# Three expert stages: router in column groups, Sinkhorn with one exponential, small loads during the norm, first weights ahead of the scatters

## The chip, the cores and the metric

The program runs on one core of a Trainium2 chip. The metric is the time of one execution on the device in microseconds. The kernel before took 3872.72 us (median of 3 runs, 3868.19 to 3879.06).

The core has TensorE (PE in the profile; its weight loads PEld), VectorE (DVE), ScalarE (ACT), GpSimd (POOL) and SyncE (SP). Each runs its own list of instructions in order; semaphores order them among each other. Transfers are issued from SP and from POOL and carried by 16 DMA engines. Everything is in fp32; large products are made from operands that are split into a high and a low part.

## The reference

The input x is two sequences of 1024 tokens of 256 features. Eight layers follow, each of the form `x = x + f(layernorm(x))`: a cross attention (A), experts (B), a cross attention (C), experts (D), a cross attention (E), a self attention with experts (F), a time warping alignment (G) and soft experts (H). The change touches the three expert layers. Each has 8 experts and chooses for every token one (B) or two (D, F):

```python
# B: top 1
logits = xf @ Wg + bg
gates = softmax(logits); idx = argmax(gates)
h = gelu(einsum('th,ehi->tei', xf, W1) + b1); y = einsum('tei,eih->teh', h, W2) + b2
out = y[token, idx]
# D: top 2 of Sinkhorn gates
scores = (einsum('btd,ed->bte', x, router_w) + router_b) / max(temperature, 0.1)
for _ in range(3):
    log_alpha = log_alpha - logsumexp(log_alpha, axis=-1, keepdims=True)   # over experts
    log_alpha = log_alpha - logsumexp(log_alpha, axis=-2, keepdims=True)   # over tokens
gates = exp(log_alpha); gates = gates / (sum(gates, axis=-1) + 1e-8)
topk_vals, topk_idx = top_k(gates, 2)
topk_gates = topk_vals / (sum(topk_vals) + 1e-8)
out = x + sum_k topk_gates[k] * (relu(x @ wg[e]) * (x @ wp[e])) @ wo[e]     # e = topk_idx[k]
# F: top 2 of the logits
rw, sel = top_k(xf @ gate_w.T, 2); rw = softmax(rw)
out = sum_k rw[k] * ((silu(xf @ w1[e].T) * (xf @ w3[e].T)) @ w2[e].T)       # e = sel[k]
```

## The kernel before

x and y hold the 2048 tokens with their features on the partitions (`[128, 2, 2048]`). The program is a row of stages; between two of them all engines meet at a barrier. The layernorm of a layer is a stage of its own (`norm_stage`, four blocks of 512 tokens), the experts the next (`moe`, names B, D, F). `norm_stage` can issue DMAs given to it as `early` from SP while it computes; before, only layer H uses that.

A `moe` stage goes through these steps:

1. **Small loads.** SP issues 8 to 10 small DMAs (router weights, index constants, bias), line 779. PE waits for all of them.
2. **Router.** PE makes the logits with the tokens as weights: 16 tiles of 128 tokens, 2 halves of the features, 8 columns each (line 836). fp32 products are issued as two instructions, so that the profile shows 64. PE then transposes the tokens into token order (line 845), and ACT copies them to `y_tok` (line 1136).
3. **Choice.** DVE, one small step after another with a semaphore between them (`chain`), makes scores and the one-hot choice. Stage D runs three Sinkhorn rounds first (lines 959 to 975): maxima over experts, exponential, sum, logarithm, subtraction, then the same over tokens, with the maximum over partitions on POOL (line 802) and the sum over partitions on PE (line 850). Exponentials and logarithms are done by ACT on request (`act_does`, line 1132), in order behind its copies to `y_tok`.
4. **Places.** PE counts the choices before each token (lines 852, 853), DVE works out which slot of 256 places belongs to which expert and each token's place (lines 1004 to 1033).
5. **Scatter.** POOL writes the tokens to their places in DRAM by indirect DMAs, 16 of them in B, 32 in D and F (line 809). Ahead of them it fetches the first slot's weights (line 795), behind them the second and third; `raw` has room for 3 slots.
6. **Slots.** 15 slots in B, 23 in D and F. SP loads a slot's tokens once all scatters have landed (line 776), PE transposes them (line 863), ACT and DVE split tokens (lines 1152, 1062) and weights (lines 1161, 1068, in pieces of 1024 columns: 1 in B, 3 in D and F), PE multiplies (lines 879, 894), POOL writes the result back by indirect DMAs (line 816) and fetches the weights of the slot three ahead. Then the results are gathered and added to x.

What sets the order is the order of the code on each engine, written by hand, and the semaphores. PE transposes slots 0 and 1 before it multiplies slot 0.

Of the kernel before, what the change touches and what calls it, by code (L numbers as in the profile page):

```python
# [656 lines left out]
def moe(nc, name, kind, func, hidden, pairs, consts, x, y, t, plus):  # L657
# [21 lines left out]
    BT = BLK // P  # L679
    rounds = 3 if kind == "sinkhorn" else 0  # L680
# [3 lines left out]
    with ExitStack() as stack:  # L684
        sc = Scope(nc, stack, name)
        router_w = sc.sb("router_w", [P, C, E])
# [12 lines left out]
        if kind == "sinkhorn":  # L699
            temp_t = sc.sb("temperature", [P, 1])  # L700
            small.append((temp_t[:, :], t[f"{name}_temperature"]))
            temperature = temp_t[:, 0:1]
        score, left, index, keep, expd = (sc.sb(n, wide) for n in ("score", "left", "index", "keep", "expd"))
# [28 lines left out]
        names = """small_loaded logits_ps dve_step act_asked act_done maxima_ready maxima_all sums_ready sums_all  # L732
# [37 lines left out]
        @block.sync  # L770
        def _(sp):
            def load(i):
                if i >= LOADS:
                    sp.wait_ge(s["turned_ps"], i - LOADS + 1)
                    sp.wait_ge(s["dest_ready"], i - LOADS + 1)
                sp.dma_start(tile_in[:, i % LOADS], rows_of(slots_dram, i)).then_inc(tile_loaded[i % LOADS], 16)

            for dst, src in small:
                sp.dma_start(dst, src).then_inc(s["small_loaded"], 16)
# [12 lines left out]
        @block.gpsimd  # L792
        def _(pool):
            def fetch(i):
                pool.indirect_dma_start(out=raw[:, i % RAWS, :], out_offset=None, in_=w_rows,
                                        in_offset=bass.IndirectOffsetOnAxis(ap=row_of[:, i:i + 1], axis=0))\
                    .then_inc(raw_loaded[i % RAWS], 16)

            pool.memset(ones_n[:, :], 1.0).then_inc(s["ones_ready"], 1)
            for r in range(rounds):  # L800
                pool.wait_ge(s["maxima_ready"], r + 1)
                pool.partition_all_reduce(colv[:, 1, :], colv[:, 0, :], P, bass.bass_isa.ReduceOp.max).then_inc(s["maxima_all"], 1)
            pool.wait_ge(s["rows_ready"], 1)
            fetch(0)
            pool.wait_ge(s["slots_ready"], 1)
            pool.wait_ge(s["tok_ready"], TILES // 2)
            for k in range(K):
                for n in range(TILES):
                    pool.indirect_dma_start(out=slots_dram, in_=y_tok[:, n, :], in_offset=None,
                                            out_offset=bass.IndirectOffsetOnAxis(ap=slot_of[:, k * TILES + n:k * TILES + n + 1], axis=0))\  # L810
                        .then_inc(scattered, 16)
            def store(i):
                pool.wait_ge(s["z_ready"], i + 1)
                pool.wait_ge(s["dest_ready"], i + 1)
                for h in range(H):
                    pool.indirect_dma_start(out=made_dram, in_=z[:, i % ZS, h, :], in_offset=None,
                                            out_offset=bass.IndirectOffsetOnAxis(ap=dest_of[:, i, h:h + 1], axis=0))\
                        .then_inc(z_stored[i % ZS], 16)

            for i in range(1, SLOTS):  # L820
                if i >= RAWS:
                    pool.wait_ge(s["w_lo_ready"], PIECES * (i - RAWS + 1))
                    if biased:
                        pool.wait_ge(s["z_ready"], i - RAWS + 1)
                fetch(i)
                if i >= RAWS:
                    store(i - RAWS)
            for i in range(SLOTS - RAWS, SLOTS):
                store(i)

        @block.tensor
        def _(pe):
            pe.wait_ge(s["small_loaded"], 16 * len(small))
# [89 lines left out]
        def _(dve):  # L923
# [21 lines left out]
            dve.wait_ge(s["small_loaded"], 16 * len(small))  # L945
            dve.wait_ge(s["logits_ps"], 1)
            logits = ps[:, 0, 0:TILES * E].rearrange("p (t e) -> p t e", e=E)
            if bias is not None:
                step(dve.tensor_tensor(score[:, :, :], logits, bias.unsqueeze(1).broadcast_to(wide), ALU.add))
            else:  # L950
                step(dve.tensor_copy(score[:, :, :], logits))
            if kind == "sinkhorn":
# [3 lines left out]
                step(dve.tensor_scalar(score[:, :, :], score[:, :, :], temp[:, 1:2], None, ALU.mult))  # L956
                for r in range(rounds):

                    step(dve.tensor_reduce(rowv[:, 0, :], score[:, :, :], AX.X, ALU.max))
                    step(dve.tensor_tensor(score[:, :, :], score[:, :, :], per_token(rowv[:, 0, :]), ALU.subtract))  # L960
# [3 lines left out]
                    step(dve.tensor_tensor(score[:, :, :], score[:, :, :], per_token(rowv[:, 2, :]), ALU.subtract))  # L964

                    step(dve.tensor_reduce(grouped(colv[:, 0, :]), s4, AX.X, ALU.max))
                    dve.sem_inc(s["maxima_ready"], 1)
                    dve.wait_ge(s["maxima_all"], r + 1)
                    step(dve.tensor_tensor(s4, s4, per_expert(colv[:, 1, :]), ALU.subtract))
                    act_does()  # L970
                    step(dve.tensor_reduce(grouped(colv[:, 3, :]), by_expert(expd[:, :, :]), AX.X, ALU.add))
                    dve.sem_inc(s["sums_ready"], 1)
                    dve.wait_ge(s["sums_all"], r + 1)
                    act_does()
                    step(dve.tensor_tensor(s4, s4, per_expert(colv[:, 4, :]), ALU.subtract))
                act_does()
# [119 lines left out]
            lo(0)  # L1096
            for j in range(PIECES):
                w_lo(0, j)
            lo(1)
# [29 lines left out]
        def _(act):  # L1129
# [3 lines left out]

            for n in range(TILES // 2):
# [3 lines left out]
            for r in range(rounds):  # L1138
                answer(4 * r + 1, expd[:, :, :], score[:, :, :], ACT.Exp)
                answer(4 * r + 2, rowv[:, 2, :], rowv[:, 1, :], ACT.Ln)  # L1140
                answer(4 * r + 3, expd[:, :, :], score[:, :, :], ACT.Exp)
                answer(4 * r + 4, colv[:, 4, :], ps[:, 1, 0:G], ACT.Ln)
            if kind == "sinkhorn":
                answer(4 * rounds + 1, expd[:, :, :], score[:, :, :], ACT.Exp)
# [39 lines left out]
            hi(0)  # L1184
            for j in range(PIECES):
                w_hi(0, j)
            hi(1)
# [1281 lines left out]
def program(nc, t, out):  # L2469
# [5 lines left out]
    with ExitStack() as stack:  # L2475
# [36 lines left out]
        norm_stage(nc, "nB", consts, norm_jobs(x, y))  # L2512
        moe(nc, "B", "top1", ACT.Gelu, D, 1, consts, x, y, t, [])
# [3 lines left out]
        norm_stage(nc, "nD", consts, norm_jobs(x, y))  # L2517
        moe(nc, "D", "sinkhorn", ACT.Relu, 2 * D, 2, consts, x, y, t, [y])
# [5 lines left out]
        with ExitStack() as layer:  # L2524
# [6 lines left out]
            norm_stage(nc, "nF2", consts, norm_jobs(y, r, scale=lnw["ln2_w"]), rms=True)  # L2531
            moe(nc, "F", "top2", ACT.Silu, 2 * D, 2, consts, x, r, t, [y])
# [12 lines left out]
def lay_out(np, i):  # L2545
# [4 lines left out]
    def rows(w):  # L2550
        return w.reshape(-1, P, w.shape[-1]).transpose(1, 0, 2)

# [31 lines left out]
    t["B_router_w"], t["B_router_b"] = rows(i["L0_ffn_Wg"]), everywhere(i["L0_ffn_bg"])  # L2584

    experts("D", [i["L1_ffn_wg"], i["L1_ffn_wp"]], i["L1_ffn_wo"])
    t["D_router_w"], t["D_router_b"] = rows(i["L1_ffn_router_w"].T), everywhere(i["L1_ffn_router_b"])
# [4 lines left out]
    t["F_router_w"] = rows(i["L2_ffn_gate_w"].T)  # L2592
# [69 lines left out]
```

## Time and profile before

| | |
|---|---|
| median of 3 runs | 3872.72 us (3868.19 to 3879.06) |
| the profiled execution | 3867.78 us, span 3865.9 us |
| mean granted clock of TensorE | 0.873 of 2.4 GHz |
| PE, DVE, ACT, POOL busy | 2975.2, 2120.6, 1513.0, 1001.7 us |
| stage B from its first small load to the end of its weights' use | 1203.4 to about 1376 us |
| stage D, the same | 1583.5 to about 1937 us |
| stage F, the same | 2804.3 to about 3130 us |
| norm ahead of stage D | 1561.7 to 1583.2 us |
| the 23 slots of stage D (lines 879, 894) | 1705.6 to 1936.5 us |
| router products (line 836) | 64 in each stage, 13.8 us in each |
| stretches before the first expert product | 61.5 us in B, 122.1 us in D, 94.4 us in F |

The profiled execution's own time is 1.9 us over its span. The last row is the time from the first small load to the first product of line 879. A fetch or scatter is an indirect DMA that POOL issues; its row on POOL is the issuing, not the transfer. Row times are counted from the start of the span. A timeline row is start, duration, engine, line, operation and operands; what stands in brackets is the idle time of the engine before it and what ended it.

### The profile page before, as it was taken

The numbers are of one execution on the slowest core, as the hardware profiler recorded it, in microseconds if no ns is written. First come the engines' busy times: TensorE is split into PE (matmuls) and PEld (weight loads), VectorE is DVE, ScalarE is ACT, GpSimd is POOL, SyncE is SP. The second block draws the span as 40 slices with busy tenths as digits, with TensorE's granted clock in tenths as the row PEclk, the third lists the DMA queues.
The fourth block names the chain that finished last, engine by engine and source line by source line (L and its number), as shares of the span: only waits on it lengthen the run. The fifth ranks groups of instructions, "written<-read, shape, count | busy, mean of one in ns | idle before, by whom it ended". The sixth has DMA issues, their size and how long they took to land. (4 is left out here: it accounts for less than half of the span.)

```text
span 3865.9 us, 43438 instructions
## 1 busy us (share of the span) xinstructions
PE 2975.2 (77%) x15086; PEld 1758.0 (45%) x15086; DVE 2120.6 (55%) x3884; ACT 1513.0 (39%) x2113; POOL 1001.7 (26%) x600
## 2 busy tenths in 40 slices
PE   4899999999994668439978599899629961049989
PEld 1545454545443542339942233333229950024457
DVE  3656555555532434338725378788327836853365
ACT  2344444444442423326523245555505630012254
POOL 1356565655572310043300100000133311001100
PEclk7899999999996788669988689999859985569999
DMA  2020000000020420045410000000025621000060
GB/s 72 5 64 7 6 6 2 4 6 6 0 66 30 150 61 1 3 151 218 174 58 1 11 4 1 6 5 2 1 106 196 217 76 17 4 22 18 37 218 22
DMA packets 87114, 198.34 MB, mean 51 GB/s; under 512 B 20387, under 2 KB 62755, under 8 KB 78880
## 3 DMA queue, kind: packets, MB, share of 16 engines
q0 software_dynamic: 18480, 108.86, 7.8%
q1 hardware_dynamic: 64608, 83.27, 7.2%
q10 hardware_dynamic: 3856, 3.95, 0.5%
q8 instruction: 105, 1.72, 0.2%
q14 instruction: 65, 0.53, 0.0%
HBM read 146.02 MB, written 49.76 MB: 51 GB/s over the span
## 5 line engine op out<-in xcount | busy, mean ns | idle before, releaser
L621 POOL TENSOR_TENSOR A_key_sums<-A_key_sums,A_probs 128x1024 f32<-128x1024 f32 (+1 forms) x224 | 526.9, 2371 | 228.1 <-ACT A_probs L514 228.1
L514 ACT ACTIVATE A_probs<-A_banks 128x512 f32<-128x512 f32 (+1 forms) x576 | 329.1, 597 | 384.7 <-PE A_banks L434 382.4
L564 DVE TENSOR_REDUCE A_part_max<-A_banks 128x1 f32<-128x367 f32 x768 | 354.1, 530 | 156.9 <-PE A_banks L355 155.6
L1844 DVE TENSOR_REDUCE F_part_max<-F_banks 128x1 f32<-128x512 f32 x512 | 325.3, 685 | 61.7 <-PE F_banks L1697 59.0
L1790 ACT ACTIVATE F_probs<-F_banks 128x1024 f32<-128x1024 f32 x256 | 248.3, 1023 | 240.5 <-PE F_banks L1743 240.3
L383 PE MATMUL A_banks<-A_probs,A_v_tok 128*64 128x512 f32 x1152 | 278.7, 605 | 0.0
L432 PE MATMUL A_banks<-A_q_one,A_k_one 128*128 128x512 f32 (+1 forms) x576 | 255.5, 444 | 26.2 <-ACT A_probs L514 23.1
L355 PE MATMUL A_banks<-A_k_one,A_q_one 128*128 128x368 f32 x768 | 230.3, 383 | 6.8 <-ACT A_v_tok L494 6.5
L184 POOL TENSOR_SCALAR F_r<-F_r,F_ln_w 128x512 f32<-128x512 f32 x16 | 28.8, 1812 | 783.0 <-DVE F_r L149 783.0
L434 PE MATMUL A_banks<-A_q_two,A_k_two 128*128 128x512 f32 (+1 forms) x576 | 227.1, 394 | 0.0
L355 PEld LDWEIGHTS A_banks<-A_k_one,A_q_one 128*128 128x128 f32 x768 | 147.3, 192 | 94.6 <-DVE A_part_max L564 58.5
L2122 PE MATMUL G_banks<-G_path_rows,G_ctx_hi 77*128 77x512 f32 x8 | 5.2, 645 | 226.0 <-DMA G_path_rows<-align_path 226.0
L432 PEld LDWEIGHTS A_banks<-A_q_one,A_k_one 128*128 128x128 f32 (+1 forms) x576 | 106.0, 184 | 139.0 <-issue 97.2
L1697 PE MATMUL F_banks<-F_k_split,F_q_split 64*128 64x512 f32 x512 | 157.3, 489 | 7.6 <-DVE F_part_max L1844 5.8
L2283 POOL TENSOR_TENSOR H_diff<-H_logits 128x512 f32<-128x512 f32 x32 | 40.7, 1272 | 426.8 <-DVE H_logits L2259 415.6
L309 PE MATMUL A_banks<-g_y,A_wqkv 128*128 128x512 f32 x256 | 121.9, 621 | 30.7 <-DVE A_part_max L604 26.0
L1710 PE MATMUL F_banks<-F_probs,F_v_tok 128*32 128x512 f32 x1024 | 143.0, 632 | 2.1 <-ACT F_probs L1790 1.9
L621 POOL TENSOR_TENSOR A_key_sums<-A_probs 128x1024 f32<-128x1024 f32 x32 | 76.0, 2375 | 261.7 <-ACT A_probs L514 261.7
L879 PE MATMUL F_banks<-F_y_hi,F_w_split 128*128 128x256 f32 x736 | 129.6, 289 | 14.4 <-DVE F_w_split L1068 14.4
L879 PE MATMUL D_banks<-D_y_hi,D_w_split 128*128 128x256 f32 x736 | 129.2, 288 | 14.4 <-DVE D_w_split L1068 14.4
L1743 PE MATMUL F_banks<-F_q_split,F_k_split 64*128 64x512 f32 x512 | 131.5, 464 | 11.0 <-ACT F_probs L1790 5.7
L1697 PEld LDWEIGHTS F_banks<-F_k_split,F_q_split 64*128 64x128 f32 x512 | 72.2, 195 | 134.0 <-DVE F_part_max L1844 102.2
(577 smaller groups left out, 6357.8 us busy)
## 6 DMA issues: line engine op xcount, KB each, us to landing
Hm_staged<-in_H_w SPq DMA_DIRECT2D x6, 1024.0 KB, 5.5
moe_in_D<-A_zeros SPq DMA_DIRECT2D x1, 6003.0 KB, 25.8
moe_in_F<-A_zeros SPq DMA_DIRECT2D x1, 6003.0 KB, 25.3
D_tile_in<-moe_in_D SPq DMA_DIRECT2D x23, 261.0 KB, 5.1
F_tile_in<-moe_in_F SPq DMA_DIRECT2D x23, 261.0 KB, 5.1
H_phi<-in_H_w SPq DMA_DIRECT2D x5, 1024.0 KB, 5.6
H_w<-in_H_w SPq DMA_DIRECT2D x5, 1024.0 KB, 4.9
D_y_tok<-moe_out_D SPq DMA_DIRECT2D x8, 512.0 KB, 5.5
```

The costliest lines, as they stand in the source:

```text
L355: pe.matmul(ps[:, MAX_BANKS[i % 3], 0:PW], q_one[:, b, j, qt * P:(qt + 1) * P], k_one[:, b, j, (i % 3) * PIECE:(i % 3) * PIECE + PW], star ...
L383: mm = pe.matmul(ps[DH * j:DH * j + DH, 4 + blk, :], v_tok[:, b, kt, DH * j:DH * j + DH], probs[:, j, kt % RING, blk * BLK:(blk + 1) * BLK ...
L432: pe.matmul(ps[0:kw, half % 3, :], k_one[:, b, j, kt * P:kt * P + kw], q_one[:, b, j, cols], start=True, stop=False)
L434: pe.matmul(ps[0:kw, half % 3, :], k_two[:, b, j, kt * P:kt * P + kw], q_two[:, b, j, cols], start=False, stop=True).then_inc(s["score_ps" ...
L514: act.activation(probs[0:kw, j, kt % RING, blk * BLK:(blk + 1) * BLK], ps[0:kw, half % 3, :], ACT.Exp, scale=1.0 / 8.0).then_inc(s["exp_re ...
L564: dve.tensor_reduce(part_max[:, i // 3, i % 3:i % 3 + 1], ps[:, MAX_BANKS[i % 3], 0:PIECE], AX.X, ALU.max).then_inc(s["piece_max"], 1)
L621: pool.tensor_tensor(key_sums[0:kw, j, :], before, probs[0:kw, j, kt % RING, :], ALU.add).then_inc(s["summed"], 1)
L879: mm = pe.matmul(ps[:, 1 + pairs * (n % 2) + pair, at * SLOT:(at + 1) * SLOT], weight_in(i, w_part, pair, c, QM * q + at), part[:, i % 2, ...
L1697: mm = pe.matmul(bank, q_split[rr, b, qt * P // BLK, hd // 2, qt * P % BLK:qt * P % BLK + P], k_split[rr, b, hd // 2, kb * BLK:(kb + 1) * ...
L1710: mm = pe.matmul(ps[V0 * hd:V0 * hd + V0, 7, :], v_tok[:, b, kt, V0 * hd:V0 * hd + V0], probs[:, i % RING, hd, :], start=kt == 0, stop=kt ...
L1790: act.activation(probs[:, i % RING, heads_at, :], ps[:, heads_at, :], ACT.Exp, scale=DH ** -0.5).then_inc(s["exp_ready"], 1)
L1844: op = dve.tensor_reduce(part_max[:, maximum_at(hd, qt), kb:kb + 1], bank, AX.X, ALU.max)
```

## The change

In all three expert stages:

- **Small loads** are handed to the norm stage ahead, whose SP block issues them. For this `moe` now calls the norm itself.
- **Router.** The weights are now `router_w`, padded from 8 to 32 columns, and the tokens are streamed, 512 columns at a time. The four blocks of tokens go to four column groups of the array and so to four groups of 32 partitions of one bank. The logits then stand as expert by token; ACT copies them to SBUF, and PE turns them with four transposes, which stand behind the first four token transposes.
- **Sinkhorn** (D). The maxima over experts and over tokens are subtracted once, one exponential is taken, and the three rounds divide by sums (reciprocal and product on DVE). One request to ACT and one to POOL are left.
- **First weights.** POOL fetches slots 0 and 1 ahead of the scatters and slot 2 in the middle of them. ACT and DVE split slot 0's weights before they wait for the first tokens. POOL's fetch of slot 3 then needs only this split (and in B, as before, the first result).

The core of the diff:

```diff
@@ moe, scope
+        small_loaded = sc.sem("small_loaded")
+        norm([(dst, src, small_loaded) for dst, src in small])
@@ POOL
-            for r in range(rounds):
-                pool.wait_ge(s["maxima_ready"], r + 1)
+            if rounds:
+                pool.wait_ge(s["maxima_ready"], 1)
                 pool.partition_all_reduce(colv[:, 1, :], colv[:, 0, :], P, bass.bass_isa.ReduceOp.max).then_inc(s["maxima_all"], 1)
             pool.wait_ge(s["rows_ready"], 1)
-            fetch(0)
+            for i in range(RAWS - 1):
+                fetch(i)
             pool.wait_ge(s["slots_ready"], 1)
             pool.wait_ge(s["tok_ready"], TILES // 2)
             for k in range(K):
                 for n in range(TILES):
+                    if k * TILES + n == KT // 2:
+                        fetch(RAWS - 1)
...
-            for i in range(1, SLOTS):
-                if i >= RAWS:
-                    pool.wait_ge(s["w_lo_ready"], PIECES * (i - RAWS + 1))
+            for i in range(RAWS, SLOTS):
+                pool.wait_ge(s["w_lo_ready"], PIECES * (i - RAWS + 1))
@@ PE
-            for n in range(TILES):
-                for c in range(C):
-                    mm = pe.matmul(ps[:, 0, n * E:(n + 1) * E], y[:, c, n * P:(n + 1) * P], router_w[:, c, :],
+            for c in range(C):
+                for g in range(NBLK):
+                    mm = pe.matmul(ps[g * ER:(g + 1) * ER, 0, :], router_w[:, c, :], y[:, c, g * BLK:(g + 1) * BLK],
                                    start=c == 0, stop=c == C - 1)
-            mm.then_inc(s["logits_ps"], 1)
+            mm.then_inc(s["by_expert_ps"], 1)
             for n in range(TILES // 2):
+                if n == 1:
+                    pe.wait_ge(s["by_expert_ready"], 1)
+                    for i in range(BT):
+                        mm = pe.transpose(ps[:, 1, i * P:(i + 1) * P], logits_t[:, i * P:(i + 1) * P], consts["ident"][:, :])
+                    mm.then_inc(s["logits_ps"], 1)
@@ DVE, Sinkhorn
+                dve.wait_ge(s["maxima_all"], 1)
+                step(dve.tensor_tensor(s4, s4, per_expert(colv[:, 1, :]), ALU.subtract))
+                act_does()
                 for r in range(rounds):
                     step(dve.tensor_reduce(rowv[:, 1, :], expd[:, :, :], AX.X, ALU.add))
-                    act_does()
...
+                    step(dve.reciprocal(rowv[:, 2, :], rowv[:, 1, :]))
+                    step(dve.tensor_tensor(expd[:, :, :], expd[:, :, :], per_token(rowv[:, 2, :]), ALU.mult))
+                    step(dve.tensor_reduce(grouped(colv[:, 3, :]), e4, AX.X, ALU.add))
                     dve.sem_inc(s["sums_ready"], 1)
                     dve.wait_ge(s["sums_all"], r + 1)
-                    act_does()
-                    step(dve.tensor_tensor(s4, s4, per_expert(colv[:, 4, :]), ALU.subtract))
-                act_does()
+                    step(dve.reciprocal(colv[:, 4, :], ps[:, 1, 0:G]))
+                    step(dve.tensor_tensor(e4, e4, per_expert(colv[:, 4, :]), ALU.mult))
@@ DVE, slots (the same on ACT with hi and w_hi)
-            lo(0)
             for j in range(PIECES):
                 w_lo(0, j)
+            lo(0)
             lo(1)
@@ ACT
+            act.wait_ge(s["by_expert_ps"], 1)
+            act.activation(logits_t[:, :], ps[:, 0, :], ACT.Copy).then_inc(s["by_expert_ready"], 1)
```

**PE in stage D, from the router to the first tokens of the slots.** `g_y` is the normed input, `D_banks` PSUM, `D_hot` the one-hot choice. Before:

```order
L836 MATMUL D_banks<-D_router_w,g_y 128x8 x32
L845 MATMUL D_banks<-g_ident,g_y 128x128 x32
L850 MATMUL D_banks<-D_colv,g_ones 128x16 x3
L852 MATMUL D_banks<-D_hot,D_tri 128x256
L853 MATMUL D_banks<-D_hot,g_ones 128x256
```

After:

```order
L841 MATMUL D_banks<-g_y,D_router_w 32x512 x8
L855 MATMUL D_banks<-g_ident,g_y 128x128 x4
L848 MATMUL D_banks<-g_ident,D_logits_t 128x128 x4
L855 MATMUL D_banks<-g_ident,g_y 128x128 x28
L860 MATMUL D_banks<-D_colv,g_ones 128x16 x3
L862 MATMUL D_banks<-D_hot,D_tri 128x256
```

Thirty-two narrow products become eight wide ones on 32 output rows, and four transposes of the logits stand between the token transposes.

**ACT in stage D, behind the copies to `y_tok`.** Before, one round (the pattern of the last five rows stands three times, and one more exponential closes it):

```order
L1136 ACTIVATE D_y_tok<-D_banks 128x2x256 x8
L1132 ACTIVATE D_expd<-D_score 128x128
L1132 ACT_TABLE_LOAD
L1132 ACTIVATE D_rowv<-D_rowv 128x16
L1132 ACT_TABLE_LOAD
L1132 ACTIVATE D_expd<-D_score 128x128
L1132 ACT_TABLE_LOAD
L1132 ACTIVATE D_colv<-D_banks 128x16
L1132 ACT_TABLE_LOAD
```

After:

```order
L1144 ACTIVATE D_logits_t<-D_banks 128x512
L1147 ACTIVATE D_y_tok<-D_banks 128x2x256 x8
L1141 ACTIVATE D_expd<-D_score 128x128
L1167 ACTIVATE D_w_split<-D_raw 128x1024 x3
L1158 ACTIVATE D_y_hi<-D_banks 128x512 x2
L1180 ACTIVATE D_active<-D_banks 128x512
```

The copy of the logits stands first, one exponential is left, no table load stands here, and slot 0's weights are split ahead of the first tokens.

**POOL in stage D, around the scatters.** `D_raw` are fetched weights, `moe_in_D` the tokens' places in DRAM, `moe_out_D` the results. Before:

```order
L799 MEMSET D_ones_n 128x256
L802 ISA
L802 ISA D_colv<-D_colv 128x16 x3
L795 DMA D_raw<-in_D_w,D_row_of 128x3072
L809 DMA moe_in_D<-D_y_tok,D_slot_of 5888x261 x32
L795 DMA D_raw<-in_D_w,D_row_of 128x3072 x3
L816 DMA moe_out_D<-D_z,D_dest_of 9984x256 x2
```

After:

```order
L806 ISA D_colv<-D_colv 128x16
L799 DMA D_raw<-in_D_w,D_row_of 128x3072 x2
L816 DMA moe_in_D<-D_y_tok,D_slot_of 5888x261 x16
L799 DMA D_raw<-in_D_w,D_row_of 128x3072
L816 DMA moe_in_D<-D_y_tok,D_slot_of 5888x261 x16
L799 DMA D_raw<-in_D_w,D_row_of 128x3072
L823 DMA moe_out_D<-D_z,D_dest_of 9984x256 x2
```

One fetch moves ahead of the scatters and one between them; one is left directly behind them.

## Rows read from the trace of the kernel before

**Rows 1.** Timeline of stage D, norm to first exponential: start, duration, engine.

```profile
1583.48 0.33 SPq L779 DMA_DIRECT2D D_router_w<-in_D_router_w  x1
...
1589.75 13.82 PE L836 MATMUL D_banks<-D_router_w,g_y 128*128 128x8 f32 x64 [14.08 <-DMA D_temperature<-in_D_temperature]
...
1603.42 5.09 PE L845 MATMUL D_banks<-g_ident,g_y 128*128 128x128 f32 x32
...
1609.58 0.28 DVE L962 TENSOR_REDUCE D_rowv<-D_expd 128x16 f32<-128x128 f32 x1 [4.24 <-ACT D_expd L1132]
```

**Rows 2.** Timeline of stages B and F: first small load, first counting product.

```profile
1203.40 0.34 SPq L779 DMA_DIRECT2D B_router_w<-in_B_router_w  x1
...
1228.49 0.39 PE L852 MATMUL B_banks<-B_hot,B_tri 128*128 128x128 f32 x2
...
2804.31 0.34 SPq L779 DMA_DIRECT2D F_router_w<-in_F_router_w  x1
...
2829.26 0.60 PE L852 MATMUL F_banks<-F_hot,F_tri 128*128 128x256 f32 x2
```

**Rows 3.** Timeline of PE in stage C: products in column groups, then full ones.

```profile
1449.56 1.06 PE L1311 MATMUL C_banks<-C_probs,C_v_tok 77*32 77x512 f32 x8
...
1452.93 1.98 PE L1277 MATMUL C_banks<-g_y,C_wq 128*128 128x512 f32 x4
```

**Rows 4.** Windows: PE, PEld, DVE, ACT, POOL busy; then clock, DMA share, GB/s.

```profile
1200.00:1203.40 3.40, 0.00 (x0) 0.00 (x0) 3.13 (x3) 0.02 (x1) 0.00 (x0) 0.52 0.00 0
...
1689.90:1700.40 10.50, 0.00 (x0) 0.00 (x0) 0.07 (x1) 0.00 (x0) 0.96 (x1) 0.50 0.95 361
```

**Rows 5.** Line 1132's table loads in the whole program.

```profile
L1132 ACT ACT_TABLE_LOAD  x12: 1283/1283/1283, 1609.6 to 1628.2; - x12
```

**Rows 6.** Timeline of stage D: a column sum in round 1, and the end of the rounds.

```profile
1613.26 0.38 DVE L971 TENSOR_REDUCE D_colv<-D_expd 128x16 f32<-128x128 f32 x1 [0.43 <-ACT D_expd L1132]
...
1614.54 0.18 ACT L1132 ACTIVATE D_colv<-D_banks 128x16 f32<-128x16 f32 x1
...
1629.87 0.29 DVE L977 TENSOR_REDUCE D_rowv<-D_expd 128x16 f32<-128x128 f32 x1 [1.23 <-ACT D_expd L1132]
```

**Rows 7.** Timeline of stages D and B: scatters and a fetch beside DVE's additions.

```profile
1640.67 1.19 POOL L795 DMA_INDIRECT D_raw<-in_D_w,D_row_of  x1 [14.77 <-DVE D_row_of L1013]
...
1645.85 4.63 DVE L1038 TENSOR_TENSOR g_x<-g_x,g_y 128x1024 f32<-128x1024 f32 x4
...
1646.03 1.94 POOL L809 DMA_INDIRECT moe_in_D<-D_y_tok,D_slot_of  x1 [4.17 <-DVE D_slot_of L1033]
...
1277.98 1.45 POOL L795 DMA_INDIRECT B_raw<-in_B_w,B_row_of  x1 [20.63 <-DVE B_z L1091]
```

**Rows 8.** Timeline of stage D, last scatter to first product.

```profile
1688.74 0.98 POOL L795 DMA_INDIRECT D_raw<-in_D_w,D_row_of  x1 [0.30 <-issue]
1689.92 30.14 SPq L776 DMA_DIRECT2D D_tile_in<-moe_in_D  x6
...
1700.44 1.94 PE L863 MATMUL D_banks<-g_ident,D_tile_in 128*128 128x128 f32 x8 [62.61 <-DMA D_tile_in<-moe_in_D]
...
1702.19 0.69 DVE L1062 TENSOR_TENSOR D_y_lo<-D_banks,D_y_hi 128x512 fp32r<-128x512 f32 x1 [1.04 <-ACT D_y_hi L1152]
...
1705.55 0.79 PE L879 MATMUL D_banks<-D_y_hi,D_w_split 128*128 128x256 f32 x2 [3.17 <-DVE D_w_split L1068]
```

**Rows 9.** Timeline of stage B, the same place, and landing times of line 776.

```profile
1256.63 22.52 SPq L776 DMA_DIRECT2D B_tile_in<-moe_in_B  x7
...
1260.87 1.09 PE L863 MATMUL B_banks<-g_ident,B_tile_in 128*128 128x128 f32 x4 [31.77 <-DMA B_tile_in<-moe_in_B]
...
DMA to landing us min/median/max: 2.7/2.9/6.7
```

**Rows 10.** Landing times of the weight fetches: stage D, then stage B behind its scatters.

```profile
DMA to landing us min/median/max: 6.9/7.5/10.1
...
DMA to landing us min/median/max: 4.6/5.6/6.9
```

More of the change, by code:

```diff
@@ L654, in top_experts, with moe @@
             step(dve.tensor_tensor(left[:, :, :], index[:, :, :], keep[:, :, :], ALU.add))
-def moe(nc, name, kind, func, hidden, pairs, consts, x, y, t, plus):
+def moe(nc, name, kind, func, hidden, pairs, consts, x, y, t, plus, norm):
     K = 1 if kind == "top1" else 2
@@ L679, in moe @@
     BT = BLK // P
+    ER = P // NBLK
     rounds = 3 if kind == "sinkhorn" else 0
@@ L943, in grouped @@
                 return v.rearrange("p (b e) -> p b e", b=B)
-            dve.wait_ge(s["small_loaded"], 16 * len(small))
+            dve.wait_ge(small_loaded, 16 * len(small))
             dve.wait_ge(s["logits_ps"], 1)
-            logits = ps[:, 0, 0:TILES * E].rearrange("p (t e) -> p t e", e=E)
+            logits = ps[:, 1, :].rearrange("p (i g e) -> p g i e", g=NBLK, e=ER)[:, :, :, 0:E]
+            by_block = score[:, :, :].rearrange("p (g i) e -> p g i e", g=NBLK)
             if bias is not None:
-                step(dve.tensor_tensor(score[:, :, :], logits, bias.unsqueeze(1).broadcast_to(wide), ALU.add))
+                step(dve.tensor_tensor(by_block, logits, bias.unsqueeze(1).unsqueeze(1).broadcast_to([P, NBLK, BT, E]), ALU.add))
             else:
-                step(dve.tensor_copy(score[:, :, :], logits))
+                step(dve.tensor_copy(by_block, logits))
             if kind == "sinkhorn":
@@ L1137, in _ @@
                                ACT.Copy).then_inc(s["tok_ready"], 1)
[L1138 to L1142, printed above, removed]
             if kind == "sinkhorn":
-                answer(4 * rounds + 1, expd[:, :, :], score[:, :, :], ACT.Exp)
+                answer(1, expd[:, :, :], score[:, :, :], ACT.Exp)
             if kind == "top2":
@@ L2530, in program @@
             self_attention(nc, consts, y, r, t)
[L2531 to L2532 removed]
+            moe(nc, "F", "top2", ACT.Silu, 2 * D, 2, consts, x, r, t, [y],
+                lambda early: norm_stage(nc, "nF2", consts, norm_jobs(y, r, scale=lnw["ln2_w"]), rms=True, early=early))
         norm_stage(nc, "nG", consts, norm_jobs(x, y))
@@ L2551, in rows, with router @@
         return w.reshape(-1, P, w.shape[-1]).transpose(1, 0, 2)
+    def router(w):
+        return np.pad(rows(w), ((0, 0), (0, 0), (0, P // NBLK - E)))
     def column(v):
@@ L2583, in lay_out @@
             np.broadcast_to(i["L0_ffn_b2"][:, None, :], (E, P, D)))
-    t["B_router_w"], t["B_router_b"] = rows(i["L0_ffn_Wg"]), everywhere(i["L0_ffn_bg"])
+    t["B_router_w"], t["B_router_b"] = router(i["L0_ffn_Wg"]), everywhere(i["L0_ffn_bg"])
     experts("D", [i["L1_ffn_wg"], i["L1_ffn_wp"]], i["L1_ffn_wo"])
-    t["D_router_w"], t["D_router_b"] = rows(i["L1_ffn_router_w"].T), everywhere(i["L1_ffn_router_b"])
+    t["D_router_w"], t["D_router_b"] = router(i["L1_ffn_router_w"].T), everywhere(i["L1_ffn_router_b"])
     t["D_temperature"] = everywhere(i["L1_ffn_temperature"])
@@ L2591, in lay_out @@
     experts("F", [i["L2_ffn_w1"].transpose(0, 2, 1), i["L2_ffn_w3"].transpose(0, 2, 1)], i["L2_ffn_w2"].transpose(0, 2, 1))
-    t["F_router_w"] = rows(i["L2_ffn_gate_w"].T)
+    t["F_router_w"] = router(i["L2_ffn_gate_w"].T)
     t["c_half"] = np.tile(np.repeat(np.eye(2, dtype=np.float32), 16, axis=0), (4, 1))
```

41 lines of the change are left out of this document (17 added, 24 removed).

## The prediction

> **What bounds the kernel now.** The views were read in this order: the page, for the shares of the engines; the timelines of the three expert stages, for what follows what ahead of the slots; the windows, for clock and DMA; and the landing times of the DMAs. PE is busy most of the span, but the change touches little of what keeps it busy. Its places lie where one engine works and the others wait: from the end of the norm to the first expert product, 122.1 us in D, 94.4 us in F, 61.5 us in B by the table. Every instruction there is a link of one chain, and a barrier closes each stage, so a microsecond saved there is saved in full unless a neighbour is late next. The reader is to see four links in D: nothing but small loads for 6.3 us, then 13.8 us of router products [rows 1]; 20.3 us from the first exponential to the end of the rounds [rows 1, 6]; a line of scatters on POOL; and 10.5 us from the first load of a slot to the first transpose, 5.1 us more to the first product [rows 8]. The slots behind them keep their code and are taken as unchanged.
>
> **Small loads.** SP's first small load leaves at 1583.48 and PE starts at 1589.75 [rows 1]. In the norm, some 20 us long, SP has nothing else to do, so the 10 issues are hidden. PE starts at about 1583.5, called T below.
>
> **Router.** Before, 64 narrow instructions take 13.82 us, 0.216 us apart [rows 1]. After, there are 8 products of 512 columns, 16 instructions. In stage C four products with 32 output rows each, 8 instructions, begin 0.89 us ahead of what follows (their row spans 1.06 us with the last one's tail), while 4 instructions of full width take 1.98 us [rows 3], some 0.43 us each without the tail. So 8 grouped instructions take the time of two wide ones: the four column groups run side by side. That was at the high level of the clock. After the norm the granted clock is 0.52 before PE starts [rows 4], so at 1.2 GHz the 16 instructions take four times 0.86, 3.4 us. Bounds: 1.7 us if the clock were high; 13.7 us if the groups did not overlap at the low clock (a rival below). I take 3.4, since the clock falls in the same idle stretch.
>
> What is added is ACT's copy and four transposes. A wait of 0.25 and a copy of 0.6 end at T + 4.3. The four transposes at 0.16 to 0.21 us (32 take 5.09 us, [rows 1]) end at T + 5.2, and DVE has logits at T + 5.5.
>
> **What is late next, stage D.** DVE's way to the exponential is 8 steps of some 0.3 us and POOL's maximum, to T + 8.8. ACT is behind: its request stands behind eight copies to `y_tok` of 0.6 us, the second of which needs tokens transposed after the logits. It ends between T + 10.5 (clock high, ACT's 0.6 us a copy the bound) and T + 12.2 (clock low, 0.86 us a pair of tiles). First sum at T + 10.9 to T + 12.6, taken 11.6. Before it was T + 26.1 [rows 1]. **D gains 14.5** (13.5 to 15.2).
>
> **B and F.** There the chain goes to the counting products, 25.1 us after the first small load in B and 24.95 in F [rows 2]. In B they stand in PE's list behind the token transposes, after at T + 9 to T + 11.2, taken 10.3: **14.8**. In F the choice takes DVE 15 steps of 0.33 us from the logits, 5 us, so T + 10.7 to T + 11.3, taken 10.8, and I take off 0.5 for counting products that may meet the low clock: **13.6**.
>
> **Rounds of D.** Before, from 1609.58 to 1629.87 [rows 1, 6], 20.3 us, with 12 table loads of 1.28 us [rows 5]. After, a round is a sum, a reciprocal and a product (0.3 each with the gap behind it, [rows 6]), a sum over tokens until the sum over partitions can be read (1.28 as from L971 to ACT's reading, [rows 6]), a reciprocal of 0.29 and a product of 0.43: 2.93 us, 8.8 for three. The exponential and the logarithm had alternated and made the loads; one exponential is left and the norm's last function is one too. **D gains 11.5** (10.5 to 12).
>
> **Scatters.** The two fetches ahead fall into the 5 us in which POOL waits for DVE's places, so the second is hidden. The fetch in the middle is not: 0.98 and a gap of 0.30 [rows 8], 1.28 us. Then there is DVE. Its four additions from 1645.85 take 4.63 us, and the scatter of 1646.03 beside them takes 1.94 us, where a fetch alone takes 0.98 [rows 7, 8]. Two such scatters stood there. Slot 0's split, 3 pieces of 1.2 us, now comes right behind these additions, while POOL still scatters; a fetch beside such a piece in B took 1.45 [rows 7]. At half speed 3.6 us cost 1.8 (0 to 1.9). **D and F lose 3.1 each; B,** with one piece, **loses 1.9.**
>
> The row rests on two-operand additions from SBUF, of 1.94 against 0.97. The Trainium skill, "SBUF — State Buffer", section "Who interferes with whom", says that such a `tensor_tensor` takes only the shared read interface, and infers from that that it does not hold up the descriptors that GpSimd writes. By that rule the split would cost the scatters nothing and the time would be 4 us shorter; the trace here speaks against it, and I go by the row.
>
> The transfers themselves are covered: between the first fetch and the last scatter lie 47 us, in which at 361 GB/s [rows 4] 17 MB could move; three fetches of 1.57 MB and 4.3 MB of scattered tokens are 9 MB.
>
> **First tokens.** Before, two fetches are issued at the end of the scatters, beside the first load, which needs 10.5 us from 1689.92; DMA is at 0.95 and 361 GB/s [rows 4, 8]. That is 3.8 MB: both fetches and the loads, so the first tokens land only when both fetches are through. After, one fetch stands there, slot 3's, since slot 0's weights are split long before. Its 1.57 MB and the tile's 0.27 at 361 GB/s are 5.1 us, taken 5.3. Bounds are 2.9 us, B's median landing [rows 9], and 8. **D gains 5.2, F,** which repeats it, **5.0.** In B slot 3's fetch still waits for the first result, so the load is alone: 4.24 us before, 2.9 after [rows 9], **1.3**.
>
> **First product.** Before, it waits 5.1 us from the first transposes for two pieces of weights [rows 8]. After, it waits for the tokens' low part, which ended at 1702.88: **2.6 in D, 2.6 in F.** In B the same count gives 1.5; slot 1's transposes stand ahead of the product, so I take **1.0**.
>
> **The sum.** Start and router 14.5 + 13.6 + 14.8 = 42.9; rounds 11.5; scatters -8.1; first tokens 11.5; first product 6.2: 64.0 us. The profiled execution took 3867.78 us, so it would take 3803.8. It is 4.9 under the median of the three runs. From the median the same sum gives 3808.7. I take 3808. Its own range: all low ends together give 50 us, 3820 from 3870; all high ends 75, 3794. So 3794 to 3821.
>
> **Rivals.**
>
> *The column groups do not overlap.* Stage C's products have 77 rows of weights, these 128, and fp32 needs two instructions each. Then 16 instructions at 0.86 us are 13.7 instead of 3.4, 10.3 lost in each stage: 3839. For it: no row shows 128 rows. Against: rows 3 show fp32 in four groups in one bank. Chance 0.08.
>
> *The tokens' way is hardly shortened.* The fetch of slot 3 is issued ahead of SP's first load, and the first load then still lands late; the fetch in the middle pushes scatters back. The first tokens gain nothing (-11.5) and the scatters lose 3 more in each of D and F: 3826. For it: before, the load was held back by whole fetches. Against: half the bytes. Chance 0.12.
>
> *The change doesn't do what it says in the rounds.* If table loads stay between copy, exponential and the slots' function, 1.28 each, D keeps three or four: 3812. Rows 5 put all 12 in line 1132, and copies in between made none. Chance 0.03, inside the first case's range.
>
> *Slower: weights ahead block POOL.* Place: the scatters in POOL's list behind fetches whose descriptors are still in the queue. If there were no room for a scatter's descriptors until a fetch has landed, each of three fetches would stop the line for its landing, up to 10.1 us in D and F [rows 10] and 6.9 in B: 81 us lost against 64 won, 3890. At the medians, 7.5 and 5.6 [rows 10], the loss is 62 us, about even; from there on it decides. Against: the scatter at 1646.03 was issued 5.4 us after the fetch of 1640.67 [rows 7], inside its landing time, and took no longer than DVE's additions explain. Chance 0.02.
>
> **How the numbers follow.** The forecast has 0.75, with the third rival 0.78; groups 0.08, tokens 0.12, slower 0.02. The forecast's own range reaches to 3821. The token case at 3826 lies near and is taken in, and most of the group case with it: 3792 to 3836 leaves out less than 2 in 10. This measurement can't tell less than 0.3%, 12 us, from no change. Faster by more 0.96, within it 0.02, slower by more 0.02.
>
> **What would show it.** Right: the router's row is some 3.4 us for 16 instructions and starts within 0.5 us of the norm's end; no table load in Sinkhorn, and rounds of 2.9 us; two fetches ahead of `slots_ready`, three or four scatters of 1.9 us in D instead of two; the first transposes 5 us after the first load; the first product 2.5 us behind them; the slots as long as before, 231 us in D. Wrong: a router row of 7 us or more, a first load above 8 us, scatters of 2 us all along, or slots that grew by as much as was saved ahead of them.

## Result and profile after

The changed kernel took 3800.81 us (median of 4 runs, 3797.79 to 3805.84) against 3874.16 for the kernel before (4 runs): ratio 0.9816, 95% interval 0.9801 to 0.9831, which is 65 to 77 us saved. In a later series it was 0.9806 (0.9785 to 0.9828). The forecast was 3808.

The profiled execution after took 3805.84 us, 61.9 under that of before. In the page PE's instructions fell from 15086 to 14954, ACT's from 2113 to 2092; the shares hardly moved. What tells is a table by stretch, each from one first or last PE instruction to the next (us). The two columns on the right are a second trace of each kernel. "Slots" are the products of all slots of a stage, from the first to the last; "attention E" holds the norm ahead of it:

| stretch | before | after | before again | after again |
|---|---|---|---|---|
| B: start of the norm to first expert product | 83.2 | 64.7 | 83.1 | 64.3 |
| D: the same | 143.9 | 112.6 | 144.1 | 111.9 |
| F: end of the norm's PE work to first expert product | 113.8 | 96.6 | 113.7 | 96.0 |
| slots of B, D, F | 108.1, 230.9, 230.9 | 106.9, 230.1, 230.7 | 109.0, 230.2, 230.7 | 107.7, 231.1, 230.4 |
| attention E | 162.7 | 168.9 | 163.5 | 168.9 |
| attention of F, up to the end of its last norm | 653.9 | 650.9 | 654.3 | 650.0 |
| gather behind the slots of D, F | 31.8, 33.8 | 33.7, 35.8 | 32.2, 33.8 | 34.2, 32.4 |

The first three rows fell by 18.5, 31.3 and 17.2 us, 67.0 in all, and repeat within 0.8 us. The others wander by microseconds.

Timeline of stage D after, from the router to the first rounds (start, duration, engine; answers to [rows 1, 6]):

```profile
1565.73 3.64 PE L841 MATMUL D_banks<-g_y,D_router_w 128*32 128x512 f32 x16 [7.86 <-PEq L104]
...
1571.87 3.54 ACT L1147 ACTIVATE D_y_tok<-D_banks 128x512 f32<-128x512 f32 x7 [0.81 <-PE D_banks L855]
...
1575.62 0.29 DVE L978 TENSOR_REDUCE D_rowv<-D_expd 128x16 f32<-128x128 f32 x1 [1.14 <-ACT D_expd L1141]
...
1583.76 0.29 DVE L986 TENSOR_REDUCE D_rowv<-D_expd 128x16 f32<-128x128 f32 x1
```

The router's 64 instructions of 13.8 us are 16 of 3.6. DVE waits for ACT's seven last copies, as forecast, and the three rounds lie between the last two rows: 8.14 us instead of 20.3. Stage B, the row that answers to [rows 2]:

```profile
1213.51 0.39 PE L862 MATMUL B_banks<-B_hot,B_tri 128*128 128x128 f32 x2
```

It stands 7.9 us behind the router's first product (19.5 before). The clock in that place, in windows (columns as in [rows 4]): B before, B after in two windows, D after.

```profile
1209.00:1223.00 14.00, 14.00 (x66) 14.00 (x67) 0.09 (x1) 0.00 (x0) 0.00 (x0) 0.50 0.00 1
...
1205.60:1209.20 3.60, 3.60 (x17) 0.68 (x17) 0.00 (x0) 0.00 (x0) 0.20 (x1) 0.50 0.01 2
...
1210.50:1214.00 3.50, 3.50 (x34) 3.42 (x31) 1.84 (x6) 3.06 (x8) 0.00 (x0) 1.00 0.00 0
...
1571.00:1575.00 4.00, 3.45 (x30) 3.21 (x28) 2.26 (x8) 3.19 (x8) 0.40 (x1) 0.95 0.01 4
```

After, the router runs at 0.50 granted, 1.2 GHz, and the token transposes mostly at 2.4: in B the grant rose 4.0 us after PE's first router product. Before, it rose 18.5 us after it, at 1227.4, when the token transposes were nearly done.

Timeline of POOL and DVE in stage D at the scatters (answers to [rows 7]), then the end of the scatters to the first product (answers to [rows 8]):

```profile
1594.55 1.19 POOL L799 DMA_INDIRECT D_raw<-in_D_w,D_row_of  x1 [20.49 <-DVE D_row_of L1022]
...
1596.03 0.94 POOL L799 DMA_INDIRECT D_raw<-in_D_w,D_row_of  x1 [0.30 <-issue]
...
1599.73 4.63 DVE L1047 TENSOR_TENSOR g_x<-g_x,g_y 128x1024 f32<-128x1024 f32 x4
1599.90 1.94 POOL L816 DMA_INDIRECT moe_in_D<-D_y_tok,D_slot_of  x1 [2.93 <-DVE D_slot_of L1042]
...
1604.28 3.49 DVE L1077 TENSOR_TENSOR D_w_split<-D_raw,D_w_split 128x1024 fp32r<-128x1024 f32 x3
1604.38 1.96 POOL L816 DMA_INDIRECT moe_in_D<-D_y_tok,D_slot_of  x1 [0.30 <-issue]
...
1608.92 0.97 POOL L816 DMA_INDIRECT moe_in_D<-D_y_tok,D_slot_of  x1 [0.30 <-issue]
...
1645.92 0.99 POOL L799 DMA_INDIRECT D_raw<-in_D_w,D_row_of  x1 [0.30 <-issue]
1647.26 23.96 SPq L782 DMA_DIRECT2D D_tile_in<-moe_in_D  x6
...
1653.92 1.94 PE L873 MATMUL D_banks<-g_ident,D_tile_in 128*128 128x128 f32 x8 [62.21 <-DMA D_tile_in<-moe_in_D]
```

Two fetches lie ahead of the scatters at no cost: the first scatter starts 10.3 us behind the counting product in D, as before. Four scatters, two of them between the rows shown, take 1.93 to 1.97 us (two of 1.9 before); the first load takes 6.7 us (10.5 before). Between 1647.2 and 1653.9 DMA moved 331 GB/s.

### The profile page after: what moved, and what is told of

It is laid out like the page before. It is cut to its first block and busy times, and to the rows that moved or that the text cites. A ratio compares the mean times of both kernels' runs of the same rounds, so it can differ in the third digit from the quotient of the medians.

```text
span 3804.0 us, 43141 instructions
## 1 busy us (share of the span) xinstructions
PE 2949.8 (78%) x14954; PEld 1718.2 (45%) x14954; DVE 2119.6 (56%) x3882; ACT 1495.8 (39%) x2092; POOL 1004.3 (26%) x598
## 5 line engine op out<-in xcount | busy, mean ns | idle before, releaser
L355 PE MATMUL A_banks<-A_k_one,A_q_one 128*128 128x368 f32 x768 | 230.2, 382 | 6.8 <-ACT A_v_tok L494 6.4
L355 PEld LDWEIGHTS A_banks<-A_k_one,A_q_one 128*128 128x128 f32 x768 | 147.3, 192 | 94.8 <-DVE A_part_max L564 58.6
L889 PE MATMUL F_banks<-F_y_hi,F_w_split 128*128 128x256 f32 x736 | 129.7, 289 | 11.8 <-DVE F_w_split L1077 10.8
L889 PE MATMUL D_banks<-D_y_hi,D_w_split 128*128 128x256 f32 x736 | 129.2, 288 | 11.8 <-DVE D_w_split L1077 10.8
```

The costliest lines, as they stand in the source:

```text
L355: pe.matmul(ps[:, MAX_BANKS[i % 3], 0:PW], q_one[:, b, j, qt * P:(qt + 1) * P], k_one[:, b, j, (i % 3) * PIECE:(i % 3) * PIECE + PW], star ...
L889: mm = pe.matmul(ps[:, 1 + pairs * (n % 2) + pair, at * SLOT:(at + 1) * SLOT], weight_in(i, w_part, pair, c, QM * q + at), part[:, i % 2, ...
```

## Experiments

The stretches are read as in the table above. "Up to the tokens" is from the counting product (`hot`) to the first transpose of a slot's tokens: 64.6 us in D and 64.3 in F before, 64.3 and 64.5 after.

**1. The kernel before once more.** No edit.

> The kernel before once more, for a second trace of it. Theory L (local): the change saves only on the chain from the norm to the first expert product (B 18.5, D 31.3, F 17.2 us between the first two traces, 67 in all); everything else that differed between them (attention E 6.2 us longer after, the gather tails of D and F 1.9 and 2.0 longer, self attention 3.0 shorter) is the granted clock's run to run wander. Then the stretch from the norm to the first product repeats within 0.5 us here (83.2 in B, 143.9 in D, 113.8 in F) and E differs from 162.7 by microseconds. Theory O (others too): the change altered the stages around; then E and the tails stand here at 162.7, 31.8 and 33.8 us within 1 us.

3867.84 us. The columns "before again" above: the three stretches repeat within 0.2 us, and E with 163.5 moved by 0.8.

**2 to 4. One part of the change each, on the kernel before.** The edits are the parts of the diff shown ahead: `norm(...)` with the small loads and the router; the Sinkhorn; POOL's fetches and the order of `w_hi`, `w_lo` ahead of `hi(0)`, `lo(0)`.

> The kernel before with the small loads in the norm and the router in column groups, and nothing else. Theory L: counting product of B 17.2 us earlier than before relative to the norm's start, D's first sum of exponentials 16.2, F's counting product 14.9: 48 us in all, about 3826. Rival: the gain needs the shorter Sinkhorn or the early weights behind it, then less than 40 us.

> The kernel before with the Sinkhorn by sums alone. Theory L: D's rounds 8.1 us instead of 20.3, 12.2 us in all, about 3862, no table load at the exponential's line. Rival: the column maximum now stands ahead of the exponential and takes 1.5 us of it back, if ACT's copies do not hide it: 10.5 us.

> The kernel before with the early fetches and the early split of slot 0's weights alone. Theory L: D and F lose 3.3 us on the scatters, win 3.8 on the first load and 2.6 at the first product, 3 us each; B loses 1.3 on the scatters, wins 1.3 and 1.3: 1 us. In all 7 us, about 3867. Rival of the prediction, that DVE's split slows scatters in all stages: four scatters of 1.9 us in D and F, and one in B; by theory L's trace B has none.

| | median | ratio (95%) | B | D | F, up to the first product |
|---|---|---|---|---|---|
| 2 loads and router | 3816.83 us | 0.9873 (0.9853 to 0.9893) | 66.2 | 126.8 | 98.7 |
| 3 Sinkhorn | 3859.35 us | 0.9976 (0.9966 to 0.9986) | 83.8 | 132.1 | 113.7 |
| 4 weights | 3859.11 us | 0.9977 (0.9967 to 0.9986) | 81.7 | 141.5 | 111.1 |

The kernel before stood at 3866.96 us (18 runs) in this series, so by the medians the parts save 50.1, 7.6 and 7.9 us, 65.6 together. By the stretches they save 49.3 (17.1, 17.1, 15.1), 11.8 in D, and 6.6 (1.5, 2.3, 2.8). Their sum is 67.7, the whole change's 67.0: no part leans on another. Experiment 2 also has E at 163.8, so the new router does not make E slow.

**5. The changed kernel once more.**

> The changed kernel once more. Theory L: B, D and F from the norm to the first product 64.7, 112.6 and 96.6 us again within 0.5; E comes back from 168.9 towards 163 us, and the whole is 67 us under before plus what the clock makes, 60 to 75. Theory O: E stays at 168.9.

3798.11 us, ratio 0.9806. The three stretches repeat within 0.8 us, but E stays at 168.9, which theory O had said. Experiments 2, 6, 7, 11 and 12 hold the same new router and show 163.8, 162.7, 163.5, 165.7 and 165.9, experiment 8 shows 168.8, and experiment 3, with the old router, 165.6; so the 168.9 is no cost of the change as such.

**6. Three fetches ahead.**

```diff
-            for i in range(RAWS - 1):
+            for i in range(RAWS):
                 fetch(i)
...
-                    if k * TILES + n == KT // 2:
-                        fetch(RAWS - 1)
```

> The changed kernel with slot 2's fetch ahead of the scatters too, instead of in the middle. If the fetch in the middle costs only its 1.28 us of POOL: D and F 1.3 us shorter from the counting product to the first tokens (63.0 for 64.3, 63.2 for 64.5), B 0.3, 3 us in all. Rival (the slower rival of the prediction, fetches in the queue hold up the scatters): the first scatters take more than 2 us each and the stretch grows.

3792.95 us, 0.9796 (0.9772 to 0.9821), which the time alone can't tell from the changed kernel's 0.9806. Up to the tokens D 63.0, F 63.3, B 31.8: 1.3, 1.2 and 0.6 less than in the changed kernel's first trace, 1.3, 0.4 and 0.2 less than in its second. The line of scatters itself, from the first to the end of the last, is the cleaner reading: 44.4 us in D and F against 45.7 in both of those traces. In D and F the third fetch is hidden before the places are known; in B it is not, the first scatter starts 1.0 us later. In D the third fetch took 12.7 us to land, and the first scatter was issued 2.6 us behind it and took the usual 1.94: no scatter waits for a fetch to land, and the slower rival falls.

**7. Slot 0's split behind the scatters.**

```diff
+            dve.wait_ge(scattered, scattered_before + 16 * KT)
             for j in range(PIECES):
                 w_lo(0, j)
             lo(0)
```

> The changed kernel, but DVE splits slot 0's weights only when all scatters have landed, so beside the first load and not beside the scatters; slot 3's fetch, which waits for that split, then also leaves behind the first load. If DVE's split slows scatters and slot 3's fetch slows the first load: two slow scatters instead of four (2.0 us less), first load 2.9 us instead of 6.7, so D and F 58.5 and 58.7 us instead of 64.3 and 64.5, first product still 2.6 behind; 11.6 us in all. Rival (the first load is slow for another reason, three tile loads in one queue): only the 2.0 come, 4 us in all. Second rival: the split is now late, first product more than 3.5 us behind the first transposes.

3783.25 us, 0.9775 (0.9754 to 0.9796). D 58.7, F 58.6 up to the tokens, first product 2.6 behind: the theory's numbers, and no run of it was as slow as the fastest of experiment 5. Timeline of this kernel in D:

```profile
1601.38 1.94 POOL L816 DMA_INDIRECT moe_in_D<-D_y_tok,D_slot_of  x1 [2.94 <-DVE D_slot_of L1042]
...
1605.87 0.97 POOL L816 DMA_INDIRECT moe_in_D<-D_y_tok,D_slot_of  x1 [0.30 <-issue]
...
1646.93 6.52 SPq L782 DMA_DIRECT2D D_tile_in<-moe_in_D  x5
...
1649.84 1.94 PE L873 MATMUL D_banks<-g_ident,D_tile_in 128*128 128x128 f32 x8 [56.65 <-DMA D_tile_in<-moe_in_D]
...
1650.71 0.98 POOL L799 DMA_INDIRECT D_raw<-in_D_w,D_row_of  x1 [5.58 <-DVE D_w_split L1077]
...
1652.43 0.77 PE L889 MATMUL D_banks<-D_y_hi,D_w_split 128*128 128x256 f32 x2 [0.65 <-DVE D_y_lo L1071]
```

Two scatters of 1.94 us are left, beside the additions; the one of 1605.87 starts when these are over. DVE's split starts at 1646.94, with the first load. Slot 3's fetch leaves 3.8 us behind that load, which now takes 2.9 us instead of 6.7. The two effects come from one edit and are told apart by these rows: 2.0 us on the scatters, 3.8 on the load.

**8. Both, and the additions in slots 3, 7, 11 and 15.** Edits 6 and 7, and DVE's four additions of y to x stand behind `lo(i + 2)` of those slots.

> The changed kernel with all fetches ahead, the split behind the scatters, and DVE's four additions of y to x moved from the scatters into slots 3, 7, 11 and 15. Theory: no scatter above 1 us; D and F 1.3 + 5.8 + 1.9 = 9 us shorter up to the first tokens, B 0.3: 18 us in all, if the slots hide the additions (D's slots 230 us). Rival: DVE is late in the slots, each addition of 1.22 us shows, and D's and F's slots grow by up to 4.9 us each: 8 to 10 us in all.

3784.59 us, 0.9773 (0.9753 to 0.9793). Up to the tokens 55.5 and 54.7, no scatter above 1.02 us, which shows that the additions made the last two of 1.94 us. But the slots took 233.4 and 233.9 us instead of 230 to 231: of 4.9 us of additions about 3 show. The rival was right in kind. By its time (5 runs) the kernel is no better than experiment 7.

**9, 10. An idle stretch ahead of attention E.** Five or fourteen memsets of DVE between two barriers.

> The changed kernel with an idle stretch of 1 to 3 us (five memsets of DVE on a spare buffer between two barriers) just ahead of attention E. E took 162.7 and 163.5 us in both traces of the kernel before and 168.9 in both of the changed one, but 163 to 164 in the variants that differ from it by some microseconds. Phase theory: what differs is when E starts against the switching of the granted clock; then E with the shift is not tied to 168.9 and may fall to 163, and attention F (650.0 and 650.9, before 653.9 and 654.3) moves too. Theory O (the change made E slower): E stays within 0.5 us of 168.9.

> The same with 14 memsets, 4 to 7 us. Phase theory: E again somewhere between 162 and 170 us, not the same as with the small shift necessarily. Theory O: 168.9.

3807.69 and 3812.25 us. The idle stretches came out longer than meant, 3.8 and 9.7 us. E took 168.7 and 166.4. In the small shift the total hides two changes: the norm took 24.7 us instead of 21.8, and the attention behind it 144.0 instead of 147.0. Over all 14 traces, E split in this way, with the mean granted clock in the attention:

| attention of E without its norm | granted | traces |
|---|---|---|
| 140.9 to 141.9 us | 0.85 | before, 1, 2, 4, 6, 7 |
| 142.8 to 144.0 us | 0.83 | 3, 9, 10, 11, 12 |
| 147.0 to 147.1 us | 0.81 | after, 5, 8 |

So the same instructions take longer where the granted clock is lower (time by grant is about 119 us in every group), and that accounts for the 6 us; neither end of the table belongs to one router. With an idle stretch ahead of E its attention was 3 and 4 us shorter than in the changed kernel. What makes the grant fall where it does stayed open. E with its norm lay between 162.7 and 168.9 us and the attention of F between 644.0 and 654.3.

**11. The router's loops swapped.**

```diff
-            for c in range(C):
-                for g in range(NBLK):
+            for g in range(NBLK):
+                for c in range(C):
```

> The changed kernel with the router's loops swapped: both halves of the features for one column group, then the next group. If neighbours in PE's list overlap only where they go to different column groups: the two halves of one group, four instructions of 0.43 or 0.86 us, run one after the other, and the row takes more than 7 us instead of 3.6 (up to 13.7 at the low clock), so B from router to counting product about 12 us instead of 7.9. If the array overlaps whatever groups are in flight with some depth: still 3.6 to 5.

3795.76 us in one run. The row of this kernel in B, to be set beside 3.64 us in B of the changed kernel; the granted clock is 0.50 in both:

```profile
1205.96 3.67 PE L841 MATMUL B_banks<-g_y,B_router_w 128*32 128x512 f32 x16 [7.86 <-PEq L104]
```

Nothing changed: from router to counting product 7.9 us in B. In both orders the 16 instructions start four at a time, 0.8 us apart. So overlap does not need neighbours in the list that go to different column groups; why is open, since a row does not tell an instruction's group (not tried: all products to one group).

**12. The best version.** Edits 6 and 7, and the additions behind the last slot:

```diff
             leave(SLOTS - 1)
+            if plus:
+                last = (SLOTS - 1) % ZS
+                dve.wait_ge(z_stored[last], stored_count(last))
+            for n in range(NBLK):
...
```

> The changed kernel with three fetches ahead, slot 0's split behind the scatters, and the additions of y to x behind the last slot, after its results have landed and while DVE waits for the gathered tokens. Theory: up to the first tokens as with all three (D 55.5, F 54.7, B 31.8 us), slots back at 230.5 instead of 233.5, and the tails of D and F no longer than before (31.8 to 35.8 us), since PE's first gathered product comes 10 us behind the last slot: 18 us under the changed kernel by the stretches, about 3780. Rival: the additions are late in the tail and it grows by 2 to 4 us in each.

3779.54 us, 0.9759 (0.9743 to 0.9775), the lowest median; the intervals of experiments 7 and 8 overlap it, so that it is the best is not shown by time. Up to the first product D 103.8, F 87.0, B 64.2; slots 231.1 and 230.8; tails 34.3 and 36.1, within 0.6 us of those of the changed kernel's first trace. F's tail was 32.4 in its second, but the additions are not what holds the tail: they end 9.7 us behind the start of the last slot's last product, PE's first gathered product comes at 10.5 in F and 11.0 in D, and DVE's next addition at 17.2 or later. Against the changed kernel's first trace the stretches save 18.9 us, against its second 17.1. Beside experiment 8, whose stretch up to the first product it shares within 0.8 us, the slots are back.

## Why the prediction was right

The sum was 64.0 us; the stretches gave 67.0, and the medians 73 with 65 to 77 as their interval. The step that counts, that a microsecond saved ahead of the slots is saved in full, held: the slots kept their 230 to 231 us, and experiments 2 to 4 add up. That the sum came so close is in part luck: the router's term was 5.4 us too small, the first tokens' term 2.9 too large. Term by term, in us:

| term | forecast | measured |
|---|---|---|
| start and router, B, D, F | 14.8, 14.5, 13.6 | 17.2, 16.2, 14.9 |
| rounds | 11.5 | 12.15 |
| scatters, B, D, F | -1.9, -3.1, -3.1 | -1.3, -3.3, -3.3 |
| first tokens, B, D, F | 1.3, 5.2, 5.0 | 1.3, 3.9, 3.4 |
| first product, B, D, F | 1.0, 2.6, 2.6 | 1.4, 2.5, 2.5 |

The forecast's 13.6 for F had 0.5 taken off for counting products at the low clock. In the changed kernel's first trace F's way from the counting product to the first scatter did grow by 0.5 us, with the granted clock at 0.50 instead of 1.00; that 0.5 stands in no row of the table.

*Start and router* was mis-sized, 5.4 us too small. The router itself was right (3.4 forecast, 3.6). The error lies behind it. I had taken the middle between transposes at the low and at the high clock, and ACT's copies at their duration of 0.6; the clock was high soon after the router (the windows of the changed kernel above), and seven copies took 3.54 us, 0.51 each. Both are beyond my favourable end.

*Rounds*: 2.7 us each instead of 2.93. The table loads are gone, as forecast; DVE reads the sum 0.93 us after it starts the reduction in the first round and 1.14 in the other two, not 1.28, which was ACT's way to it.

*Scatters*: the long scatters in D were forecast and experiments 7 and 8 show both causes apart. A "piece" is one DVE instruction of 1024 columns with two inputs in SBUF. In B no scatter was long, although one lay beside a piece. Rows of B, first of the changed kernel, then of experiment 10, where the piece came first by chance:

```profile
1222.27 0.97 POOL L816 DMA_INDIRECT moe_in_B<-B_y_tok,B_slot_of  x1 [0.30 <-issue]
1222.41 1.23 DVE L1077 TENSOR_TENSOR B_w_split<-B_raw,B_w_split 128x1024 fp32r<-128x1024 f32 x1 [2.93 <-ACT B_w_split L1167]
...
1221.78 1.22 DVE L1077 TENSOR_TENSOR B_w_split<-B_raw,B_w_split 128x1024 fp32r<-128x1024 f32 x1 [2.73 <-ACT B_w_split L1167]
1221.85 2.00 POOL L816 DMA_INDIRECT moe_in_B<-B_y_tok,B_slot_of  x1 [0.30 <-issue]
```

A scatter that starts 0.14 us ahead of the piece takes 0.97 us, one that starts 0.07 us behind it 2.00. In all 14 traces every long scatter started while a piece was running, 0.07 us or more behind its start, and ended 0.8 to 0.9 us behind its end, also one of B in experiment 6 that started late in its piece and took 1.18. So the cost is not half speed, which the prediction had, but a wait for the piece to end: it goes by the number of scatters that meet a running piece, and that explains the missing one in B. One scatter lies at the border: in B of experiment 9 it started 0.04 us behind the piece and took 0.97, and there the piece took 1.29 instead of 1.22. The Trainium skill, "SBUF — State Buffer", section "Who interferes with whom", infers that a `tensor_tensor` does not hold up GpSimd's writing of descriptors; 1.94 against 0.97 us speaks against that for these scatters. The same section says that a `tensor_tensor` with both inputs in SBUF contends with GpSimd's reads, and the scatters do read `slot_of` from SBUF; which access it is, no run here shows. Its rule that issue order decides who blocks agrees with the two orders in B as far as the scatter goes; the piece that came second in the rows above was hardly held up, at 1.23 us.

*First tokens*: the direction was right, the rival of the late tokens (gain nothing) was wrong, and the truth lay between, nearer to the forecast. The load alone takes 2.9 us, and one fetch ahead of it adds 3.8 (experiment 7), less than its 1.57 MB at 361 GB/s would take, 4.4 us. What the forecast of 5.3 left out was not bytes: it priced the load at its 0.27 MB, 0.7 us, where the load alone takes 2.9 us.

*The other 6 us* of the medians against the stretches lie inside the interval. E's 6 us loss, which goes with the granted clock there, and the shorter attention in F are not accounted for by any term of mine, and I don't claim them for the change.

Of the rivals, groups that do not overlap would have shown a router row of 13.7 us; it is 3.6. Table loads in the rounds: none. POOL blocked by its queue: experiment 6 put one more fetch ahead, and the line of scatters in D and F was 1.3 us shorter, with no scatter there longer than before.

## What to carry to other kernels

Ahead of a long loop, look for stretches in which one engine works and the rest wait: what is shortened there is saved in full, and the terms can be checked one by one from the start of one stage to the next. Work that is moved into such a stretch should be placed by what it disturbs as well: DVE instructions with two SBUF operands doubled the indirect DMAs of POOL that started under them, and a bulk fetch issued just ahead of the load that everyone waits for cost 3.8 us; one wait that put DVE's split and the fetch behind the scatters and the load saved 11.5 us up to the tokens of D and F, more than the whole reordering of weights with its 6.6. Before a difference of the whole is explained, take a second trace and read the granted clock of each stage: here stages that nobody touched moved by 6 to 10 us.

## What was not expected of the hardware

- 16 fp32 instructions of 512 columns on 32 output rows take 3.6 to 3.7 us at 1.2 GHz with the four blocks in either order (3.64 and 3.67 in B); rows of 3.4, as in F after, are those in which the clock rose before the last four ended.
- An indirect DMA on POOL that starts while a DVE instruction with two SBUF inputs runs ends 0.8 to 0.9 us behind the end of that instruction (1.94 us instead of 0.97 where it starts early in it); one that starts 0.14 us before it takes 0.97. DVE is hardly slowed, by 0.07 us at the most (1.29 in experiment 9): four additions take 4.63 us beside POOL's scatters and, in experiment 12, with POOL idle.
- E, with the same code, took 162.7 to 168.9 us in 14 traces. Its attention took 141, 143 to 144 or 147 us at a mean granted clock of 0.85, 0.83 or 0.81. What sets the grant there stayed open.
